# Rows of the two f16 parts of h W 260 words long instead of 264, so that low parts start at an odd multiple of 8 bytes

## The reference

```python
h = relu(layernorm(x))
Wh = h @ W_w + W_b                                   # 8192 x 256
e = leaky_relu((Wh @ a1)[:, None] + (Wh @ a2)[None, :], negative_slope=0.2)
attention = softmax(where(adj > 0, e, -9e15), axis=1)   # 8192 x 8192
out = x + attention @ Wh
```

## Time and profile before

| | |
|---|---|
| median of 3 runs | 1465.53 us |
| the profiled execution | 1465.83 us |
| its span, first to last instruction | 1464.0 us |
| TensorE (matmuls) busy | 98% |
| VectorE busy | 98% |
| ScalarE busy | 77% |
| GpSimd busy | 63% |
| TensorE's granted clock, mean | 0.997 of full |

### The profile page before, as it was taken

How to read it: one execution, slowest core, us unless ns; L and a number is a source line. 1 busy time by engine, 2 the same in 40 slices (tenths; PEclk the granted TensorE clock), 3 DMA queues, 4 the chain that set the end, 5 groups by cost and what they waited for, 6 DMA issues and landing times.

```text
span 1464.0 us, 30087 instructions
## 1 busy us (share of the span) xinstructions
PE 1435.3 (98%) x12702; PEld 1270.6 (87%) x12702; DVE 1430.7 (98%) x1254; ACT 1123.1 (77%) x1096; POOL 920.9 (63%) x1232
## 2 busy tenths in 40 slices
PE   6989999999999999999999999999999999999998
PEld 4868888888888888888888888888888888888887
DVE  8999999999999999999999999999999999999995
ACT  5878888787788877787788877787787877787771
POOL 4758444457965499366974589455984579556800
PEclk9999999999999999999999999999999999999999
DMA  9749977694497909996297917997097945977120
GB/s 220 84 41 96 86 54 53 45 108 38 68 102 74 85 18 100 74 98 48 56 102 73 93 26 83 84 90 63 26 112 59 109 44 62 98 75 71 46 42 30
DMA packets 179574, 107.53 MB, mean 73 GB/s; under 512 B 20080, under 2 KB 176368, under 8 KB 179440
## 3 DMA queue, kind: packets, MB, share of 16 engines
q0 software_dynamic: 163296, 82.90, 67.5%
q1 hardware_dynamic: 16144, 22.71, 5.6%
HBM read 298.45 MB, written 8.42 MB: 210 GB/s over the span
## 4 chain that ended last, share of the span: by engine, by line
PE 81%; DVE 16%; issue 2%; ACT 1%; DMA 0%; POOL 0%; SPq 0%; DVEq 0%
PE acc L925 81%; DVE work L744 4%; DVE work L737 4%; DVE adj_cols L663 2%; DVE xr L521 1%; DVE X L568 1%; PE acc L880 0%; DVE xr L532 0%; DVE xr L563 0%; DVE xr L553 0%; DVE xr L846 0%; DVE xr L557 0%; DVE xr L555 0%; DVE xr L849 0%; DVE xr L542 0%
## 5 line engine op out<-in xcount | busy, mean ns | idle before, releaser
L925 PE MATMUL acc<-X,work 128*128 128x258 f16 (+2 forms) x12288 | 1351.5, 273 | 5.4 <-DVE work L818 4.7
L925 PEld LDWEIGHTS acc<-X,work 128*128 128x128 f16 x12288 | 1203.3, 98 | 153.7 <-issue 5.3
L303 POOL DMA_DIRECT2D adj_rows<-in_adj x1024 | 555.4, 598 | 418.4 <-DVE adj_cols L663 396.1
L431 ACT ACTIVATE work<-work 128x2048 f16<-128x2048 f32 x254 | 484.3, 1911 | 185.0 <-PE acc L925 92.7
L744 DVE SCALAR_TENSOR_TENSOR work<-work 128x2048 f16<-128x2048 f32 x254 | 605.0, 2382 | 4.6 <-ACT work L431 4.5
L737 DVE SCALAR_TENSOR_TENSOR work<-work,sigma,adj_cols 128x2048 f32<-128x2048 f32 x254 | 590.3, 2326 | 3.9 <-issue 0.2
L416 ACT ACTIVATE work<-q_odd,r_j 128x1024 f32<-128x1024 f32 x256 | 279.7, 1140 | 37.5 <-DVE work L744 37.0
L416 ACT ACTIVATE work<-work,r_j 128x1024 f32<-128x1024 f32 x252 | 275.1, 1140 | 33.5 <-DVE work L744 33.1
L663 DVE STREAM_TRANSPOSE adj_cols<-adj_rows 128x512 int32<-128x512 int32 x256 | 176.2, 697 | 0.0
L318 POOL TENSOR_SCALAR part_mean<-mean_hw,rows_without_edge 128x256 f32<-128x256 f32 x56 | 167.2, 2985 | 8.6 <-POOL xr L320 8.4
L320 POOL TENSOR_TENSOR xr<-xr,part_mean 128x256 f32<-128x256 f32 x56 | 128.3, 2291 | 4.7
(11 more groups left out here) (90 smaller groups left out, 154.1 us busy)
## 6 DMA issues: line engine op xcount, KB each, us to landing
adj_rows<-in_adj POOLq DMA_DIRECT2D x1024, 64.0 KB, 7.4
xr<-in_L_gnn_W_b POOLq DMA_DIRECT2D x16, 512.0 KB, 15.1
out<-xr SPq DMA_DIRECT2D x15, 512.0 KB, 3.5
work<-in_x SPq DMA_DIRECT2D x28, 256.0 KB, 14.6
xr<-in_x POOLq DMA_DIRECT2D x14, 512.0 KB, 8.5
work<-q_rows SPq DMA_DIRECT2D x4, 512.0 KB, 6.2
q_odd<-q_rows SPq DMA_DIRECT2D x4, 512.0 KB, 6.2
work<-in_x SPq DMA_DIRECT2D x8, 128.0 KB, 3.3
```

Of the source, the lines that this page charges most:

```text
L303: pool.dma_start(rows8[QP * q:QP * (q + 1), n % R8], adj_v[s, m, k, q]).then_inc(s_rows[n % R8], 16)
L431: nc.scalar.mul(Et[:, at:at + 2, 0, :], Wt[:, i % RING], SCALE).then_inc(s_H, 1)
L925: return nc.tensor.matmul(acc[:, m, 0:WIDTH[n]], Et[:, 2 * (k % RING) + e, 1 if n == 2 else 0, m * P:(m + 1) * P], X16[:, 2 * k + e, 1 if ...
```

## The change

One number changes: the padding of each part of h W goes from 8 f16 words to 4.

```diff
@@ -42,7 +42,7 @@
     F1 = F + 1
     F2 = F + 2
 
-    FX = F + 8
+    FX = F + 4
     NB = N // P
     R = 1024
     NS = N // R
```

## The result

The change makes the kernel slower by half a per cent: 1473.62 us median of 5 runs (1472.20 to 1474.27) against 1465.5 us (five runs, 1465.42 to 1466.8) before, ratio 1.0049 with a 95% interval of 1.0038 to 1.006. The forecast was 1465.6, the range ended at 1470.2. The time lies between rival A (1468.9) and rival B (1475.4).

A forecast was written before the change was run, and what follows sets the result against it. TensorE's back-to-back matmuls were taken to bound the kernel. All terms were 0, so 1465.83 us stayed 1465.83; the runs' median lies 0.3 us lower, giving 1465.6 us. Range 1464.8 to 1470.2.

The forecast's parts named there:

- rival A: In stage 2, each low-part matmul pays 0.9 ns for one more 16-byte line: 3.3 us, 1468.9 us; chance 0.22.
- rival B: In stage 2, a start within a line costs each low part 2.65 ns more: 9.6 us, 1475.4 us; chance 0.14.
- What bounds the kernel: For 1190 of 1464 us, time is a sum of TensorE matmul distances, 109.74 ns each, in L925.
- I take 0: the transposes are nearest in size and in start: Price of L925's low-part reads at odd multiples of 8, set at 0 us from the transposes L871.
- the bounds drawn from L871 and L905: Price limits for low-part reads from stage 1 matmuls: up to 0.6 us by L871, 2.3 us by L905.
- The upper end: Highest price for low-part reads in L925, taken from L880: 1.2 ns each, 4.3 us in all.
- the lower end of rival A: Smallest price per low-part matmul in rival A, 0.64 ns, bounded from the warm-up matmuls L905.
- High parts: High-part reads in L925 now start at multiples of 16 instead of 32 bytes; priced at 0.
- other tiles: Tiles behind X move by 1024 bytes; the steady stretch showed no dependence on address, so priced at 0.
- writes into X: Stage 1 writes, 64 of them to an odd multiple of 8; bounded by 0.4 us, taken as 0.
- The signs to look for: In the gapless row, 109.74 ns distance, wrong if moved over 0.27 ns or row broken; widths stay at 273 ns.

The follow-up runs named there:

- e2: The change with high and low parts of each block exchanged, so high parts start at odd multiples of 8 bytes; 1466.26 us, ratio 1.0000.
- e3: The kernel before, with all of X 8 bytes further, so all parts start at an odd multiple of 8; 1465.66 us, ratio 1.0002.
- e4: The kernel before, with the low part of block b moved b // 8 words, so starts lie 0 to 14 bytes behind a multiple of 16; 1467.85 us.
- e5: The change with matmuls of two blocks crossed, so most low parts don't follow their own block's high part; 1466.74 us, ratio 1.0004.
- e12: The kernel before, with the high-times-high matmul reading 266 to 402 columns in passes 1 to 7 and 258 in the last; 1542.0 us.
- e6: The change with the high-times-high matmul reading 256 columns instead of 258, except the first of a pass and bank; 1464.25 us.
- e1: The change plus 1024 bytes of unused tile behind X, so all other tiles lie where they lay before; 1472.31 us, ratio 1.0044.
- e8: The kernel before, with the high-times-high matmul reading 266 columns, the last 8 into unused accumulator columns; 1487.05 us.
- e7: The kernel before with rows of 258 words and no padding, so the low part begins where the high part ends; 1472.77 us.
- e10: The kernel before, with the matmul of low weights and high part reading 256 columns instead of 257; 1463.91 us, ratio 0.9982.

## Why the prediction was wrong

- **What bounds the kernel** was read rightly: a plain sum of matmul distances, one for one. The cost came in as such a distance and nowhere else, and the 0.71 us of wait at 267 us was absorbed, as rival A had it.
- **The step that failed** is "I take 0: the transposes are nearest in size and in start". The start within a line was taken for the thing that matters, and the rows were chosen by it. Starts at an odd multiple of 8 are indeed free (e2, e3, e4), so the bounds drawn from L871 and L905 priced something that costs nothing. The price hangs on the pair, on where the read before ends and this one begins: three matmuls take 331.1 ns where the low part follows its own high part, and 329.2 ns with the same starts in another order (e5). The high part's 258 words end at byte 516, and the table of the change has the low part of block 0 at 520: the pair could be read there. A matmul's read was looked at alone, in a stream in which it never is alone.
- **The upper end** of that term, 1.2 ns, came from L880, whose excess of 2.9 ns was put down to its start. L880 is the only group of stage 1 in which a read ends in the line in which the next begins (Wx[:, 0] ends at 1032, Wx[:, 1] begins there), once in four instructions. The bound spread that once over two reads. The measured price is 1.9 ns for each low part, 6.9 us.
- **A slip in the bounds**: for L905 the prediction has (3.19 - 0.38) / 13 = 216.3 ns, but it is 216.2. The excess is then 2.8 ns and the bound 0.34 ns for one read, 1.2 us in all, not 0.64 and 2.3. Neither the forecast nor the upper end came from it, but the lower end of rival A did. With the right value L905 lay as close to L925 as the transposes did.
- **Rival A** had the right place and the right absorption, and the wrong size and reason (0.9 ns for a line more). A 33rd line alone costs nothing: in e4 low parts 4 and 8 bytes into a line touch 33 lines and take the time of 32. So the sentence of the Trainium skill, page "SBUF — State Buffer", section "Door 1: The DMA port swizzle", that lines have 16 bytes fits all runs here, though a rule in bytes would too (see e12). That each crossing pays is not borne out for these contiguous reads (e4). That two hits on a line are needed fits e4 if a hit is a pair of words, which no run tests by itself: with 8 bytes left in the first line the start is free, with 4 it costs 0.8 ns; with 2 it costs 1.6, of which 0.8 is what the other starts off a pair (2, 6 and 10 bytes) pay too.
- **Rival B** (2.65 ns) was near in time, 1475.4, by luck: its mechanism, a start within a line, is refuted by e3.
- **High parts, other tiles, writes into X**: priced at 0, and 0 they were (the high parts by e6, which has them where the change has them and pays nothing; the tiles by e1; the writes by L568 and L391 above).
- **The signs to look for** did their work: the distance moved by 0.62 ns, over the 0.27 named, and the row did not break up; it closed. That the three widths would stay at 273 ns a record was no test, since the ends of matmul records are modelled: 270 to 274 ns in both profiles says nothing of a distance that changed by 3.5 ns.

## What to carry to other kernels

When matmuls run back to back, look at where each moving operand ends and the next begins: if the next one starts inside the last three 16-byte lines of the one before, move it. Either pad the row so that it starts in a later line than the one in which the read before ended (the very next line is far enough: last byte 515, start 528 in the kernel before), or put another matmul between the two (e5). A gapless stream is read by its mean distance over thousands of matmuls, which resolves a tenth of a nanosecond; when a layout change is to be priced from a trace, choose the rows by the pair of neighbouring accesses, not by the address of one.

## What the runs showed of the hardware

- The price of two overlapping neighbours: 1.9 ns with the start in the last line or the one before it, 0.9 in the third from the end, 0 from the fourth on (e12, with the start on a line's first byte). It is paid with starts 0, 4, 8 and 12 bytes into a line (e8, e7, the change).
- Apart from that, an f16 read may start 0, 4 or 8 bytes into a line for nothing. 2, 6, 10 and 12 cost 0.8 ns, 14 cost 1.6 (e4).
- Columns count in pairs: behind 258 and 257 columns the distance is 110.0 ns, behind 256 it is 109.2, and three matmuls with 256 in place of 257 take 328.4 ns instead of 329.2 (e10). Counted in pairs, the excess in the kernel before is 2.5 ns a matmul (109.2 - 256 / 2.4), with a load of the stationary operand ahead of every one.
- The 16 warm-up instructions get the full clock in some executions and the lower level for a part of them in others, whatever the layout of X: they average 385 ns in before and e1, 511 to 513 in after, e5 and e10. In after, the matmuls of stage 2 began 1.0 us later than in before.
